# A graph layer's edge stream beside a state-space scan: PSUM banks regrouped, decays written to PSUM, row sums issued behind the turn and spread

## The chip, the cores and the metric

The kernel runs on one core of one Trainium2 chip. The metric is the device time of one launch in microseconds (us). The kernel before takes 3823.23 us, the median of 3 runs (3822.45 to 3824.71).

## What is computed

`x` is 6250 nodes by 256 features, with 200,000 edges (`src`, `dst`, sorted by `dst`). One graph layer and one mixture-of-experts layer follow each other, each with a residual. The change concerns the first layer only:

```
xn   = layernorm(x)
proj = (xn @ gat_w.T).reshape(n, 4, 64)
e    = leaky_relu(s_src[src] + s_tgt[dst], 0.2)       # four heads
exp_e= exp(e - max(e)); denom = segment_sum(exp_e, dst)
agg  = segment_sum(proj[src] * exp_e / denom[dst], dst)
perm = argsort(out_degree(src) + noise)
xz   = xn[perm] @ in_proj.T                           # -> xc, z
xc   = silu(causal_conv4(xc)); dbc = xc @ x_proj.T    # dt row, B, C
dt   = softplus(dt_row @ dt_proj.T + b)
h_t  = exp(dt * A) * h_(t-1) + (dt * xc) * B_t        # 256 channels x 16 states
y    = (h * C).sum(states) + xc * D_param;  y = y * silu(z) @ out_proj.T
```

After it come the per-node part (norms, gate, feed-forward) and the experts (`nodes`, `plan`, `experts`), which the change leaves as they are.

## The kernel before

`layers` runs two streams of work at once on the same engines.

The **edge stream** goes by *pairs* (an edge chunk of 512 edges and a tile of 128 target nodes), 440 in all. For a pair, GpSimd (POOL) issues four indirect DMAs (`gather`, L567) that bring 4 x 128 rows of 260 numbers into `G`. ScalarE (ACT) makes the one-hot of the targets (`one_hot`, L628 and L633). TensorE (PE) turns it (`turn`, L663) and spreads the tile's scores over the edges (`spread`, L670), both into PSUM bank `fl_ptx`; ACT copies them out (`keep_turned`, L643 and L644). Every fourth pair VectorE (DVE) makes the logits of four pairs (`logits`, L585 to L602), and ACT their exponentials: into the rows in SBUF (`weights`, L648) and into PSUM bank `fl_pw` (`weights_again`, L654). DVE multiplies the gathered rows by them (`scale`, L610), PE sums them per target (`gather_sums`, L683, four matmuls, eight records in the trace, into one of two banks `fl_ps0`, `fl_ps1`), and DVE adds the sum to `ACC` (`add`, L620). POOL may gather pair q once the sums of pair q-8 are made (`free`).

The **scan stream** goes by *chunks* of 224 nodes, 28 in all. A chunk has 16 *slots*, one per state. Two neighbouring states are handled together. DVE forms the inflow in the odd slot before (`inflow`, L1111, reading PSUM bank `fl_pb`), scans both states in the even slot (`scan`, L1124: 900 elements of decays `mb_dA` and inflows `mb_dB`, both in SBUF) and multiplies by C in the odd slot (`read_out`, L1134, reading `fl_pc`). ACT makes the decays of one state per slot (`decay`, L1251: two activations of 224), two states ahead, in a buffer for four states. PE copies B and C to all partitions (`copies_b` L1353 in odd slots, `copies_c` L1363 in even slots) and sums over the states (`sum_up`, L1375, odd slots).

Three slots of every four (1, 2, 3, 5, 6, 7, 9, 10, 11, 13, 14, 15 of a chunk) carry a pair; slots 0, 4, 8, 12 carry none. The logits fall in slots 1, 6 and 11. Beside that each slot prepares a part of the next chunk (`prepare`) or gives out the last (`give_out`): PE has in slot 2 the projection of z (L1382), in slot 4 the convolution (L1407), in slot 6 x_proj, in slot 8 dt, in slot 10 the output projection.

The order on each engine is written out by hand: `run` calls each engine's own `slot(M, S)` for 32 slots (two chunks), and then loops over 32-slot bodies. Every engine works through its queue in order; the engines meet through counting semaphores (`s["turned_sb"]`, `s["added"]` and so on). The edge stream starts earlier, beside the counting of degrees (36 pairs) and the ranking (56 pairs), and has 12 more pairs before the first chunk's scan.

What is handed to PE in a slot, in the kernel before, is the body of

```
def edges_tensor(pe, S):
    if not early(S.number, 2):
        gather_sums(pe, S - 2)
    turn(pe, S + GU)
    spread(pe, S + GU)
```

## Time and profile before

| | |
|---|---|
| median of 3 runs | 3823.23 us (3822.45 to 3824.71) |
| the profiled execution | 3830.27 us, its span 3828.5 us |
| busy share of the span | PE 76%, PEld 56%, DVE 70%, ACT 57%, POOL 69% |
| busy in 915 to 2868 us, the 28 chunks (1953 us) | PE 1618.89, DVE 1732.35, ACT 1406.68, POOL 1542.10 us |
| mean granted TensorE clock | 0.898 in the whole, 0.96 in that stretch |

How to read it: PEld is TensorE's loading of weights, which lies beside the matmuls. Idle time stands behind an instruction in brackets, with the event that ended it. The chain that ended last names only the experts at the end of the program, so for the stretch of the scans the engines' idle times and the timeline have to be read. POOL's spans are rough, but the starts of its instructions follow each other closely enough to be counted.

### The profile page before, as it was taken

To read this page: it belongs to the slowest core of one execution; us is meant where nothing else is said; L and a number is where in the kernel's file an instruction comes from. 1 tells how busy PE (TensorE), PEld (TensorE's weight loads), DVE (VectorE), ACT (ScalarE), POOL (GpSimd) and SP (SyncE) were. 2 spreads that over 40 slices of the span, in tenths; PEclk is the share of its full clock that TensorE was granted. 3 is DMA by queue.
4 is the path that set the end of the run, shared out by engine and by line. 5 is a ranking of instruction groups with operands and counts; after the bars stand their busy time and mean duration, and the time that the engine had idled before them with its cause. 6 is when DMAs were issued, how large, how long until landed. Compare 5 with 4: busy or idle time off the path is not lost. (4 is left out here: it accounts for less than half of the span.)

```text
span 3828.5 us, 60997 instructions
## 1 busy us (share of the span) xinstructions
PE 2897.5 (76%) x16306; PEld 2157.1 (56%) x16307; DVE 2661.2 (70%) x4225; ACT 2163.9 (57%) x4819; POOL 2649.2 (69%) x2119
## 2 busy tenths in 40 slices
PE   6465566517888788887888888888883889659998
PEld 5455455415565565565665655656652455448887
DVE  6577466625988988989888888899893788511111
ACT  2322377716777677777676776777772665412222
POOL 2788788877777777777777777777773477424443
PEclk9788777768899999999999999999996999879999
DMA  7333444454444444544444444444465243157775
GB/s 225 105 83 84 133 106 107 115 172 131 118 124 121 124 118 117 127 120 122 124 118 120 123 118 126 121 120 124 120 112 136 56 106 99 69 133 143 143 144 105
DMA packets 295783, 460.78 MB, mean 120 GB/s; under 512 B 59431, under 2 KB 217880, under 8 KB 295288
## 3 DMA queue, kind: packets, MB, share of 16 engines
q0 software_dynamic: 116320, 279.61, 30.8%
q1 hardware_dynamic: 179224, 178.73, 16.6%
q14 instruction: 180, 1.47, 0.1%
q8 instruction: 59, 0.97, 0.1%
HBM read 394.01 MB, written 63.43 MB: 119 GB/s over the span
## 5 line engine op out<-in xcount | busy, mean ns | idle before, releaser
L567 POOL DMA_INDIRECT el_g<-table,el_ix x1344 | 1546.7, 1151 | 412.4 <-issue 392.9
L683 PE MATMUL fl_ps<-el_g,el_oh 128*128 128x260 f32 x3520 | 959.0, 420 | 255.2 <-DVE el_g L610 207.2
L683 PEld LDWEIGHTS fl_ps<-el_g,el_oh 128*128 128x128 f32 x3520 | 697.3, 209 | 370.5 <-DVE el_g L610 215.1
L567 POOL DMA_INDIRECT el_g<-table,eg_src x436 | 592.8, 1360 | 155.2 <-issue 125.9
L610 DVE TENSOR_TENSOR el_g<-el_g,fl_pw 128x1024 f32<-128x1024 f32 x440 | 533.5, 1213 | 22.2 <-ACT fl_pw L654 22.1
L1124 DVE TENSOR_TENSOR_SCAN mb_h<-mb_dA,mb_zero,mb_dB 128x900 f32<-128x900 f32 x224 | 468.1, 2090 | 51.2 <-ACT mb_dA L1251 30.7
L1375 PE MATMUL fl_py<-mb_hc,ident 128*128 128x448 f32 x896 | 405.0, 576 | 0.5 <-DVE mb_hc L1134 0.5
L1251 ACT ACTIVATE mb_dA<-mb_dt,mb_a 128x224 f32<-128x224 f32 x900 | 382.7, 475 | 35.3 <-issue 21.2
L628 ACT ACTIVATE el_away<-el_dst,el_less 128x512 bf16<-128x512 bf16 x445 | 321.1, 721 | 108.3 <-DMA el_dst<-dst_rows 81.3
L2258 POOL DMA_INDIRECT out<-ex_y,ex_to x112 | 174.2, 1555 | 279.3 <-DVE ex_y L2217 254.5
L643 ACT CAST el_oh<-fl_ptx 128x512 f32<-128x512 bf16 x444 | 253.6, 571 | 190.8 <-PE fl_ptx L670 185.6
L663 PE MATMUL fl_ptx<-el_ident,el_oht 128*128 128x128 bf16 x1776 | 183.9, 230 | 183.3 <-ACT el_sx L644 167.3
L633 ACT ACTIVATE el_oht<-el_away 128x512 bf16<-128x512 bf16 x445 | 280.3, 630 | 36.2 <-issue 5.4
L663 PEld LDWEIGHTS fl_ptx<-el_ident,el_oht 128*128 128x128 bf16 x1776 | 139.5, 103 | 283.4 <-issue 155.0
L1111 DVE TENSOR_TENSOR mb_dB<-mb_u,fl_pb 128x896 f32<-128x896 f32 x225 | 242.5, 1078 | 46.8 <-PE fl_pb L1353 46.8
L2217 DVE TENSOR_TENSOR ex_y<-ex_py,ex_b 128x512 f32<-128x512 f32 x56 | 38.8, 692 | 333.0 <-PE ex_py L2179 333.0
L648 ACT ACTIVATE el_g<-el_dm 128x64 f32<-128x64 f32 x110 | 28.2, 256 | 424.6 <-DVE el_dm L601 424.4
L620 DVE TENSOR_TENSOR ACC<-ACC,fl_ps 128x260 f32 x440 | 182.7, 415 | 115.9 <-PE fl_ps L683 78.1
L1134 DVE TENSOR_TENSOR mb_hc<-mb_h,fl_pc 128x896 f32<-128x896 f32 x224 | 241.6, 1078 | 0.0
L585 DVE TENSOR_REDUCE el_s<-el_sx 128x128 f32<-128x384 f32 x110 | 67.6, 615 | 233.7 <-DMA el_g<-table,eg_src 171.3
L2232 ACT COPY ex_xt<-ex_px 128x512 f32<-128x512 f32 x56 | 32.8, 586 | 345.2 <-PE ex_px L2153 345.2
L1363 PE MATMUL fl_pc<-mb_parts,mb_sel 96*128 96x224 bf16 x448 | 84.9, 272 | 167.0 <-DVE mb_hc L1134 167.0
(306 smaller groups left out, 5509.0 us busy)
## 6 DMA issues: line engine op xcount, KB each, us to landing
el_dst<-dst_rows SPq DMA_DIRECT2D x446, 128.0 KB, 3.4
ex_w<-in_moe_W SPq DMA_DIRECT2D x56, 512.0 KB, 3.4
el_g<-table,el_ix POOLq DMA_INDIRECT x1344, 3.0
ex_x<-routed_x SPq DMA_DIRECT2D x56, 257.0 KB, 2.8
el_g<-table,eg_src POOLq DMA_INDIRECT x436, 2.8
mb_x<-sorted_x SPq DMA_DIRECT2D x30, 224.0 KB
table<-px_tr SPq DMA_DIRECT2D x7, 910.0 KB, 9.6
el_g<-in_x SPq DMA_DIRECT2D x7, 896.0 KB, 8.0
```

The source lines that it names most:

```text
L567: pool.indirect_dma_start(out=G[b // GU][:, b % GU * NJ + j, :], out_offset=None, in_=dram["table"], in_offset=bass.IndirectOffsetOnAxis(a ...
L610: nc.vector.tensor_tensor(rows, rows, weight[:, at, :].unsqueeze(3).to_broadcast([P, NJ, NH, FO]), ALU.mult).then_inc(s["scaled"], 1)
L628: nc.scalar.activation(AWAY[:], DST[:, n % 4, :], ACT.Abs, bias=LESS[:, 0:1]).then_inc(s["away"], 1)
L633: nc.scalar.activation(OHT[:, n % RO, :], AWAY[:], ACT.Relu, bias=1.0, scale=-1.0).then_inc(s["hot"], 1)
L643: nc.scalar.copy(OH[:, n % (2 * GU)], pT)
L663: nc.tensor.transpose(pT[:, j, :], OHT[:, n % RO, j * P:(j + 1) * P], I16[:])
L683: mm = nc.tensor.matmul(pS[n % 2], OH[:, n % (2 * GU), j, :], G[n // GU % 2][:, n % GU * NJ + j, :], start=j == 0, stop=j == NJ - 1)
L1111: nc.vector.tensor_tensor(dB[:, :, :, 1:], wide_u, pB[:].unsqueeze(2).to_broadcast([P, 2, KD, TC]), ALU.mult).then_inc(s["dB"], 1)
L1124: nc.vector.tensor_tensor_scan(line(H[:]), line(dA[:, n % 2 * 2:n % 2 * 2 + 2]), line(dB[:]), ZERO[:, 0:1], ALU.mult, ALU.add).then_inc(s[ ...
L1134: nc.vector.tensor_tensor(HC[:, n % 2], H[:, :, :, 1:], pC[:].unsqueeze(2).to_broadcast([P, 2, KD, TC]), ALU.mult).then_inc(s["hc"], 1)
L1251: ins = nc.scalar.activation(dA[:, n % 4, k, 1:], DT[:, n // NS % 2, k, :], ACT.Exp, scale=A[:, k, n % NS:n % NS + 1])
L1375: mm = nc.tensor.matmul(pY[:], w["ident"][:], HC[:, n % 2, r], start=first and r == 0, stop=last and r == 1)
```

## The change

- **Decays in PSUM.** The SBUF buffer `mb_dA` for four states goes. The decays of the two states of a scan are written by ACT to `pA`, two PSUM banks (`fl_pa`), with no second buffer. ACT therefore makes all four activations in the odd slot, behind `keep_last` and the slot's `prepare`, and waits for the scan before to be done. In even slots it makes none.
- **Banks.** `fl_ps0` and `fl_ps1` become one bank `fl_ps`, so the sums of a pair wait until the pair before has been added to `ACC`. The copies of C and the edge weights share `fl_pw`. PE, ACT and DVE are kept from touching this bank at the same time by waits: `copies_c` waits for the scaling (and in slot 12 for `weights_again`), `scale` in odd slots waits for the copies of C, `weights_again` waits for `read_out` or `copies_c`.
- **Order on PE.** `gather_sums` goes behind `turn` and `spread`; `copies_c` goes to the end of the even slot's edge work.
- The convolution taps, which lay in the buffer of the decays, have their own (`mb_taps`).

```diff
@@ -550,9 +550,9 @@
         pTX, words = ps("fl_ptx", [P, 512]), NJ * P // 2
         pT = pTX[:, 0:words].bitcast(BF16).rearrange("p (j e) -> p j e", e=P)
         pX = pTX[:, words:words + NJ * SPREAD].rearrange("p (j s) -> p j s", s=SPREAD)
-        pS = [ps(f"fl_ps{b}", [P, 512])[:, 0:ROW] for b in range(2)]
+        pS = ps("fl_ps", [P, 512])[:, 0:ROW]
         pW = ps("fl_pw", [P, 512])
-        weight = pW[:, 0:GU * NJ * NH].rearrange("p (c h) -> p c h", h=NH)
+        weight = pW[:, 2 * TC:2 * TC + GU * NJ * NH].rearrange("p (c h) -> p c h", h=NH)
         ACC = w["ACC"]
 
         def free(pool, p):
@@ -617,7 +617,7 @@
             if not early(q, 1):
                 dve.wait_ge(s["added"], q)
             dve.wait_ge(s["summed"], q + 1)
-            nc.vector.tensor_tensor(at, at, pS[p.n % 2], ALU.add).then_inc(s["added"], 1)
+            nc.vector.tensor_tensor(at, at, pS, ALU.add).then_inc(s["added"], 1)
 
         def one_hot(act, p):
 
@@ -676,11 +676,11 @@
             q, n = p.number, p.n
             pe.wait_ge(s["scaled"], q + 1)
             pe.wait_ge(s["turned_sb"], q + 1)
-            if not early(q, 2):
-
-                pe.wait_ge(s["added"], q - 1)
+            if not early(q, 1):
+
+                pe.wait_ge(s["added"], q)
             for j in range(NJ):
-                mm = nc.tensor.matmul(pS[n % 2], OH[:, n % (2 * GU), j, :], G[n // GU % 2][:, n % GU * NJ + j, :],
+                mm = nc.tensor.matmul(pS, OH[:, n % (2 * GU), j, :], G[n // GU % 2][:, n % GU * NJ + j, :],
                                       start=j == 0, stop=j == NJ - 1)
             mm.then_inc(s["summed"], 1)
 
@@ -700,10 +700,10 @@
                 weights_again(act, S)
 
         def edges_tensor(pe, S):
+            turn(pe, S + GU)
+            spread(pe, S + GU)
             if not early(S.number, 2):
                 gather_sums(pe, S - 2)
-            turn(pe, S + GU)
-            spread(pe, S + GU)
 
         with part:
             sb = lambda n, s_, t=F32: part.enter_context(nc.sbuf_tensor(n, s_, t))
@@ -940,15 +940,15 @@
             PARTS, MID = sb("mb_parts", [3 * 2 * NS, 2, TC], BF16), sb("mb_mid", [2 * NS, TC], BF16)
             REST = sb("mb_rest", [2 * NS, TC])
             DTR = sb("mb_dtr", [BX, TC])
-            dA = sb("mb_dA", [P, 4, KD, 1 + TC])
             dB, H = (sb(f"mb_{n}", [P, 2, KD, 1 + TC]) for n in ("dB", "h"))
             HC = sb("mb_hc", [P, 2, 2, KD, TC])
-            taps = dA[:].rearrange("p b k t -> p (b k t)")[:, 0:CONV * D].rearrange("p (j d) -> p j d", j=CONV)
+            taps = sb("mb_taps", [P, CONV, D])[:]
             XN = [t.rearrange("p b k t -> p (b k t)")[:, u * D:(u + 1) * D] for t in (dB[:], H[:], HC[:, 0]) for u in range(3)]
             H0, ZERO = sb("mb_h0", [P, N2, 2, KD]), sb("mb_zero", [P, 1])
             LOWER = sb("mb_lower", [P, 1])
             Y, O, OR = sb("mb_y", [P, KD, TC]), sb("mb_o", [P, KD, TC]), sb("mb_or", [RB, TS, D])
-            pB, pC = ps("fl_pb", [P, 2, TC]), ps("fl_pc", [P, 2, TC])
+            pB, pC = ps("fl_pb", [P, 2, TC]), pW[:, 0:2 * TC].rearrange("p (r t) -> p r t", r=2)
+            pA = ps("fl_pa", [P, 1024])[:, 0:2 * KD * (1 + TC)].rearrange("p (s k t) -> p s k t", s=2, k=KD)
             pY, pM = ps("fl_py", [P, KD, TC]), ps("fl_pm", [P, 512])
             wide = lambda t: t[:, 0:KD * TC].rearrange("p (k t) -> p k t", k=KD)
             xs = dram["sorted_x"].rearrange("(c r p) d -> c p r d", p=RB, r=TS)
@@ -1098,7 +1098,7 @@
                 dve.wait_ge(s["set"], 11)
 
                 nc.vector.memset(LOWER[:], float(-np.log(ROOT)))
-                nc.vector.memset(dA[:, :, :, 0:1], 0.0).then_inc(s["set"], 1)
+                nc.vector.memset(pA[:, :, :, 0:1], 0.0).then_inc(s["set"], 1)
 
                 def inflow(p):
 
@@ -1121,7 +1121,7 @@
                         dve.wait_ge(s["h0"], 2 * m)
                         dve.wait_ge(s["hc"], m)
                     line = lambda t: t.rearrange("p s k t -> p (s k t)")
-                    nc.vector.tensor_tensor_scan(line(H[:]), line(dA[:, n % 2 * 2:n % 2 * 2 + 2]), line(dB[:]), ZERO[:, 0:1],
+                    nc.vector.tensor_tensor_scan(line(H[:]), line(pA), line(dB[:]), ZERO[:, 0:1],
                                                  ALU.mult, ALU.add).then_inc(s["h"], 1)
 
                 def read_out(p):
@@ -1131,7 +1131,7 @@
                     if not early(m, 2):
 
                         dve.wait_ge(s["y"], m - 1)
-                    nc.vector.tensor_tensor(HC[:, n % 2], H[:, :, :, 1:], pC[:].unsqueeze(2).to_broadcast([P, 2, KD, TC]), ALU.mult
+                    nc.vector.tensor_tensor(HC[:, n % 2], H[:, :, :, 1:], pC.unsqueeze(2).to_broadcast([P, 2, KD, TC]), ALU.mult
                                             ).then_inc(s["hc"], 1)
 
                 def prepare(c, b, at):
@@ -1190,6 +1190,8 @@
                         give_out(c - 1, 1 - b)
                     if S:
                         add(dve, S - 3)
+                        if at % 2:
+                            dve.wait_ge(s["C"], two.number + 1)
                         scale(dve, S - 1)
                     steps = logits(dve, S) if S and S.n % GU == 0 else None
                     if steps:
@@ -1244,11 +1246,11 @@
                 def decay(p):
 
                     m, n = p.number, p.n
-                    if not early(m, 4):
-
-                        act.wait_ge(s["h"], two_states(p).number - 1)
+                    if not early(m, 2):
+
+                        act.wait_ge(s["h"], two_states(p).number)
                     for k in range(KD):
-                        ins = nc.scalar.activation(dA[:, n % 4, k, 1:], DT[:, n // NS % 2, k, :], ACT.Exp,
+                        ins = nc.scalar.activation(pA[:, n % 2, k, 1:], DT[:, n // NS % 2, k, :], ACT.Exp,
                                                    scale=A[:, k, n % NS:n % NS + 1])
                     ins.then_inc(s["dA"], 1)
 
@@ -1318,10 +1320,14 @@
                     if not early(c, 1):
                         give_out(c - 1, at)
                     prepare(c + 1, 1 - b, at)
-                    decay(M + 2)
+                    if at % 2:
+                        decay(M + 1)
+                        decay(M + 2)
                     if S:
                         keep_turned(act, S + GU)
                     if S and S.n % GU == 0:
+
+                        act.wait_ge(s["hc"] if at % 2 else s["C"], two_states(M).number + 1)
                         weights_again(act, S)
 
                 for k in range(SCAT):
@@ -1443,10 +1449,16 @@
                     two = two_states(M)
                     if at % 2:
                         copies_b(two + 1)
-                    else:
-                        copies_c(two)
                     if S:
                         edges_tensor(pe, S)
+                    if not at % 2:
+
+                        last = S or pair_beside(M - 1)
+                        pe.wait_ge(s["scaled"], last.number)
+                        if not S and last.n % GU == 0:
+
+                            pe.wait_ge(s["weight"], last.of(GU) + 1)
+                        copies_c(two)
                     if at % 2 and not early(M.number, 2):
                         sum_up(two - 1)
                     if not early(c, 1):
```

PE's queue in slot 2 of a chunk, in the kernel before, from the sums to the copies of B of slot 3 (`fl_ps` sums, `fl_ptx` turn and spread, `fl_pm` the projection of z, `fl_pb` copies of B):

```order
L683 MATMUL fl_ps<-el_g,el_oh 128x260 x4
L658 REGISTER_ALU
L663 MATMUL fl_ptx<-el_ident,el_oht 128x128 x4
L668 ISA
L668 TENSOR_LOAD eg_tile
L668 ISA x2
L670 ISA
L670 MATMUL fl_ptx<-eg_parts,el_oht 128x25 x4
L1382 MATMUL fl_pm<-mb_xt,mb_wi 128x224 x4
L1351 REGISTER_ALU
L1353 MATMUL fl_pb<-mb_parts,mb_sel 128x224 x2
```

The same place in the changed kernel, from slot 2's turn to the projection of z (`fl_pw` is now the copies of C):

```order
L663 MATMUL fl_ptx<-el_ident,el_oht 128x128 x4
L668 ISA
L668 TENSOR_LOAD eg_tile
L668 ISA x2
L670 ISA
L670 MATMUL fl_ptx<-eg_parts,el_oht 128x25 x4
L677 REGISTER_ALU
L683 MATMUL fl_ps<-el_g,el_oh 128x260 x4
L1457 REGISTER_ALU
L1369 MATMUL fl_pw<-mb_parts,mb_sel 128x224 x2
L1388 MATMUL fl_pm<-mb_xt,mb_wi 128x224 x4
```

The sums have moved from ahead of the turn to behind the spread, and the copies of C have moved in behind them, ahead of the projection.

ACT's queue in slots 2 and 3, in the kernel before (`el_away`, `el_oht` one-hot; `el_oh`, `el_sx` the copies of turn and spread; `mb_sz` the copy of z):

```order
L628 ACTIVATE el_away<-el_dst,el_less 128x512
L633 ACTIVATE el_oht<-el_away 128x512
L1251 ACTIVATE mb_dA<-mb_dt,mb_a 128x224 x2
L643 CAST el_oh<-fl_ptx 128x512
L644 COPY el_sx<-fl_ptx 128x100
L628 ACTIVATE el_away<-el_dst,el_less 128x512
L633 ACTIVATE el_oht<-el_away 128x512
L1239 COPY mb_h<-mb_h 128x4
L1242 COPY mb_dB<-mb_h 128x4
L1266 COPY mb_sz<-fl_pm 128x448
L1251 ACTIVATE mb_dA<-mb_dt,mb_a 128x224 x2
```

The same place in the changed kernel:

```order
L628 ACTIVATE el_away<-el_dst,el_less 128x512
L633 ACTIVATE el_oht<-el_away 128x512
L643 CAST el_oh<-fl_ptx 128x512
L644 COPY el_sx<-fl_ptx 128x100
L628 ACTIVATE el_away<-el_dst,el_less 128x512
L633 ACTIVATE el_oht<-el_away 128x512
L1241 COPY mb_h<-mb_h 128x4
L1244 COPY mb_dB<-mb_h 128x4
L1268 COPY mb_sz<-fl_pm 128x448
L1253 ACTIVATE fl_pa<-mb_dt,mb_a 128x224 x4
```

Slot 2 has lost its two activations of decays, and slot 3 has four, ahead of the copies of turn and spread.

## Rows read from the trace of the kernel before

**Rows 1.** Busy time by engine in the chunks' stretch: PE, PEld, DVE, ACT, POOL, clock, DMA

```profile
915.00:2868.00 1953.00, 1618.89 (x8927) 1169.88 (x8926) 1732.35 (x2291) 1406.68 (x3439) 1542.10 (x1340) 0.96 0.48 121
```

**Rows 2.** Groups by line, same stretch: count, busy us, mean ns, idle before

```profile
L567 POOL DMA_INDIRECT el_g<-table,el_ix x1339 | 1542.0, 1152 | 410.9 <-issue 391.4 <-PE fl_ps L683 19.5
...
L1124 DVE TENSOR_TENSOR_SCAN mb_h<-mb_dA,mb_zero,mb_dB 128x900 f32<-128x900 f32 x224 | 468.1, 2090 | 51.2 <-ACT mb_dA L1251 30.7 <-DVE mb_dB L1111 18.0 <-issue 2.3
...
L585 DVE TENSOR_REDUCE el_s<-el_sx 128x128 f32<-128x384 f32 x84 | 51.6, 615 | 23.1 <-ACT el_sx L644 14.6 <-DMA el_g<-table,el_ix 8.3
...
L1165 DVE SCALAR_TENSOR_TENSOR mb_dt<-mb_v,mb_t 128x448 f32<-128x448 f32 x28 | 17.5, 625 | 1.0
```

**Rows 3.** Timeline, a gather beside a scan and one alone: start, duration, engine

```profile
2025.38 2.08 DVE L1124 TENSOR_TENSOR_SCAN mb_h<-mb_dA,mb_zero,mb_dB 128x900 f32<-128x900 f32 x1
2025.51 2.71 POOL L567 DMA_INDIRECT el_g<-table,el_ix  x1 [0.30 <-PE fl_ps L683]
...
2028.52 0.95 POOL L567 DMA_INDIRECT el_g<-table,el_ix  x1 [0.30 <-issue]
```

**Rows 4.** Groups by line, POOL beside the ranking, 440 to 760 us

```profile
L567 POOL DMA_INDIRECT el_g<-table,eg_src x205 | 257.4, 1256 | 64.1 <-issue 58.5 <-PE fl_ps L683 5.6
```

**Rows 5.** Timeline, slots 0 to 6 of one chunk, three engines

```profile
2102.13 2.09 DVE L1124 TENSOR_TENSOR_SCAN mb_h<-mb_dA,mb_zero,mb_dB 128x900 f32<-128x900 f32 x1 [0.23 <-DVE mb_dB L1111]
...
2107.78 1.93 PE L683 MATMUL fl_ps<-el_g,el_oh 128*128 128x260 f32 x8
...
2108.31 0.26 ACT L648 ACTIVATE el_g<-el_dm 128x64 f32<-128x64 f32 x1 [3.64 <-DVE el_dm L601]
...
2109.11 0.85 ACT L1251 ACTIVATE mb_dA<-mb_dt,mb_a 128x224 f32<-128x224 f32 x2
...
2109.87 0.57 ACT L643 CAST el_oh<-fl_ptx 128x512 f32<-128x512 bf16 x1
...
2110.34 0.25 ACT L644 COPY el_sx<-fl_ptx 128x100 f32<-128x100 f32 x1
...
2110.47 0.24 ACT L654 ACTIVATE fl_pw<-el_dm 128x64 f32<-128x64 f32 x1
...
2110.73 0.38 PE L663 MATMUL fl_ptx<-el_ident,el_oht 128*128 128x128 bf16 x4 [1.01 <-ACT el_sx L644]
...
2117.38 2.45 PE L1407 MATMUL fl_pm<-mb_xt,mb_wc 128*128 128x224 f32 x12
...
2123.64 1.93 PE L683 MATMUL fl_ps<-el_g,el_oh 128*128 128x260 f32 x8
...
2123.84 1.09 DVE L1111 TENSOR_TENSOR mb_dB<-mb_u,fl_pb 128x896 f32<-128x896 f32 x1 [0.98 <-PE fl_pb L1353]
...
2125.41 0.39 PE L663 MATMUL fl_ptx<-el_ident,el_oht 128*128 128x128 bf16 x4
...
2125.72 0.43 DVE L620 TENSOR_TENSOR ACC<-ACC,fl_ps 128x260 f32 x1 [0.79 <-PE fl_ps L683]
...
2127.43 0.24 ACT L644 COPY el_sx<-fl_ptx 128x100 f32<-128x100 f32 x1
...
2128.00 0.62 DVE L585 TENSOR_REDUCE el_s<-el_sx 128x128 f32<-128x384 f32 x1 [0.72 <-ACT el_sx L644]
```

**Rows 6.** Timeline, slots 7 and 8 of that chunk, and the next chunk's first scan

```profile
2133.42 1.22 DVE L610 TENSOR_TENSOR el_g<-el_g,fl_pw 128x1024 f32<-128x1024 f32 x1 [0.64 <-ACT fl_pw L654]
...
2137.13 0.85 ACT L1251 ACTIVATE mb_dA<-mb_dt,mb_a 128x224 f32<-128x224 f32 x2
...
2138.02 2.09 DVE L1124 TENSOR_TENSOR_SCAN mb_h<-mb_dA,mb_zero,mb_dB 128x900 f32<-128x900 f32 x1 [1.10 <-ACT mb_dA L1251]
...
2171.22 2.09 DVE L1124 TENSOR_TENSOR_SCAN mb_h<-mb_dA,mb_zero,mb_dB 128x900 f32<-128x900 f32 x1 [0.23 <-DVE mb_dB L1111]
```

**Rows 7.** Busy time by engine in 2042 to 2046 us, columns as in Rows 1

```profile
2042.00:2046.00 4.00, 4.00 (x14) 3.27 (x13) 4.00 (x4) 3.48 (x10) 3.33 (x3) 0.57 0.52 132
```

**Rows 8.** Timeline, the sums of slot 3 in that stretch

```profile
2043.88 2.74 PE L683 MATMUL fl_ps<-el_g,el_oh 128*128 128x260 f32 x8
```

## The prediction

> **What bounds the kernel now.** The chain of waits that ended last names only the experts' part, so I read the stretch of the 28 chunks by itself: first busy time by engine, then the groups by line, then the timeline of one chunk. The stretch takes 1953 us, 69.75 us a chunk; DVE is busy for 1732, POOL for 1542, PE for 1619, ACT for 1407 [rows 1].
>
> POOL looks like a bound. Its gathers take 1542.0 us and its gaps before them 410.9, together 1953, and nearly all gaps are "issue" [rows 2]: it never waits. A gather that starts beside a scan takes 2.71 us, one alone 0.95 [rows 3], so the mean of 1152 ns is 1339 x 0.2 = 270 us above one alone. The reader is to see that POOL is blocked by the scans, and that it has no idle time to give.
>
> The question is how much DVE waits for POOL. DVE's waits for gathered rows are at L585, and "DMA" has 8.3 us there in the whole stretch [rows 2]. The rest of DVE's idle time ends with PE or ACT, or is the short step from one instruction to the next. The quiet chunk of the timeline has none of those waits for DMA and lasts from 2102.13 to 2171.22, 69.09 us [rows 5, 6]. So there are two bounds almost in one place: POOL at 69.75, and the ring of DVE, PE and ACT at 69.1. Freeing POOL gives 28 x 0.66 = 18 us at most unless the ring also gets shorter. What the change does to the ring decides.
>
> **The ring, part by part.** Times are of the quiet chunk.
>
> *Slots 1 to 5, PE's order.* Before, the sums of slot 2 (2107.78, 1.93 us) run while ACT is still behind: PE then waits 1.01 us for ACT's copy, and turns at 2110.73 [rows 5]. From that turn to the convolution at 2117.38 and on to the sums at 2123.64 PE hardly rests, and the end of this stretch is waited for: DVE's inflow at 2123.84 had waited 0.98 us for the copies of B behind the convolution [rows 5]. Now the sums of slot 2 must follow the turn. So 1.93 us of work that lay in a pause goes into the stretch that is waited for; the next instruction starts 1.77 behind the start of such sums (2123.64 to 2125.41) [rows 5], and I take 1.8. The copies of C of slot 2 go in as well: 0.2 us (a start-to-start step, as from PE's copies of B to the sums). Slots 3 and 4 have the same work in another order.
>
> *Slots 1 to 5, ACT's order.* The turn waits for ACT's copy, which ended at 2110.34 + 0.25. In slot 1 ACT had one state's decays, 0.85 us busy, the next one starting 0.76 behind (2109.11 to 2109.87) [rows 5]. Now it has two states' there, all ahead of this copy: +0.8. Together the convolution and the inflow of slot 5 come 1.8 + 0.2 + 0.8 = 2.8 us later. Behind the inflow, which reads PSUM, are slot 6's `add`, `scale` and logits in DVE's queue, and PE's next copies of C.
>
> *Slot 6.* `add` waits for sums that now follow turn and spread: +0.3 (2125.41 to the next instruction on PE). But the later gate is the logits' wait for the copies of slot 5, which stand behind the second pair of decays: +0.8 again. The read at 2128.00 came 0.3 us after the copy's end (2127.43 + 0.24) [rows 5], and I take that off: +0.5.
>
> *Slot 7.* Decays no longer stand between the logits and the edge weights. DVE's 0.64 us wait there [rows 6] goes: -0.6.
>
> *Slot 8.* The scan waited 1.10 us for decays that began at 2137.13, behind slot 7's copies [rows 6]. Both pairs are now there: +0.8. The wait at slot 2's `scale` (a second pair of decays ahead of `weights_again`) is 0.3 and lies ahead of the stretch that PE sets, so it costs nothing.
>
> *Other slots.* In slots 3, 11, 13 and 15 ACT makes the four activations (twice 0.8 us) while DVE has at least `read_out` and inflow (1.09 each), and mostly `add` and `scale` too, so the single buffer costs nothing there. The wait of `scale` for the copies of C is met: PE needs about 2.2 us after `add` for sums and copies, and DVE has `scale` and a scan, 3.3 us, between. In slot 12 the copies wait for `weights_again`; DVE's scan covers it. POOL needs sums eight pairs back, and at over 70 us a chunk it has some 9 us of slack in each, so its wait for later sums costs nothing.
>
> *PSUM operands.* ACT's 64-element exponential takes 0.24 us into PSUM and 0.26 into SBUF [rows 5]; that is nothing to 0.02 per activation, and I take 0.1 off a chunk. The Trainium skill (ScalarE: Activation LUTs, Step-by-step: what each stage is for) says that writing to PSUM is faster than writing to SBUF, without a figure for it. The trace agrees in sign; by the rule alone the sum would be lower, by the row it is lower by this 0.1. The scan's price from PSUM isn't in the trace. A DVE operation with two SBUF inputs takes 625 ns for 448 elements, 1.4 ns each, and the inflow with one in PSUM 1.09 us for 896, 1.2 ns [rows 2, 5]; the scan has 2.3 ns [rows 2]. Below: the scan falls to the inflow's rate, -1.0 us each. Above: a fixed 0.23 us more, as one dependent step of DVE costs (2102.13) [rows 5], on the five scans of eight that the ring waits for: +1.2 a chunk. I take 0: L1165 with two SBUF inputs isn't slow, so the scan's 2.3 ns is its own, and reading PSUM shows no surcharge in the inflow.
>
> Sum: 2.8 + 0.5 - 0.6 + 0.8 - 0.1 = +3.4 on 69.1, thus 72.5. I leave in the low TensorE clock that chunks have at times (below), 0.66 less POOL's share of 8.3/28 = 0.3: 72.5 + 0.35 = 72.85, or +3.1 against 69.75. 28 x 3.1 = 87 us.
>
> *Before the chunks.* 104 pairs run with the single bank and the new order. Beside the ranking POOL takes 257.4 + 64.1 us of 320, 6.3 us a pair, and almost never waits for sums [rows 4]. It may run eight pairs ahead of them, so sums a few us later cost 0; at worst 0.1 us a pair, 10 us.
>
> The profiled execution takes 3830.3 us, so 3917 by its own measure; it stands 7 us above the median of the runs, which gives 3910.
>
> **Rivals.**
>
> *POOL's blockade was the real bound (faster).* With the scan's decays in PSUM, gathers fall towards 0.95 + 0.3 us: 48 x 1.25 = 60 us a chunk. The Trainium skill (SBUF — State Buffer, Who interferes with whom) says that a VectorE instruction with at most one SBUF input, outside its two-port modes, doesn't contend with GpSimd; rows 3 agree with a blockade by an operation that has two, and by that rule it ends. For this rival speaks that POOL is full. If the ring's costs are hidden, the chunk goes from 69.75 to 69.1 or a little lower: 3823 - 18 = 3805. Its far end is DVE's busy time plus half of its idle time, 1732 + 110 = 1842, or -111: 3712. It decides as soon as the ring grows by less than 0.6 us a chunk. Against it: DVE waited only 8.3 us for gathers, and two of my terms stand on waits that exist already (0.98 and 1.10 us).
>
> *The scan itself gets faster (faster).* At -1.0 us per scan, five of eight on the ring's path: 3.1 - 5 = -1.9 a chunk, 3823 - 53 = 3770. L1165 speaks against it.
>
> *PE's clock falls in the stretch that is waited for (slower still).* PE's pause ahead of slot 2's turn grows from 1.01 us to about 3, since the sums no longer fill it. In the chunk before the quiet one the granted clock had 0.57 of full speed at that place, near the lower of TensorE's levels (1.2 of 2.4 GHz) [rows 7], and the sums took 2.74 us instead of 1.93 [rows 8]. With 0.8 for the sums and as much for the projection before them in every chunk: 3.1 + 1.6 - 0.35 = 4.35, x 28 = 122: 3945. Against it: the quiet chunk had a pause too, and kept its clock.
>
> *Only ACT's part lands.* If PE catches up by slot 5, +0.5 - 0.6 + 0.8 + 0.8 = 1.5 less 0.7 that POOL gives: 0.8 a chunk, 3846.
>
> **How the numbers follow.** Forecast 50%; clock 20%; only ACT's part 10%; POOL's blockade 16% (4 of it within 0.2%); the faster scan 4%. The forecast's own range is 3880 to 3940, for the terms of 2.8 and 0.8 may together be off by a third. The range that leaves out 2 in 10 is 3815 to 3965. A measurement of this kernel tells 0.2%, about 8 us, from no change. Faster 17%, same 5%, slower 78%.
>
> **What would show it.** Right: gathers beside scans at 0.95 us and POOL waiting for sums; DVE's wait at the inflow for the copies of B near 3 to 4 us once a chunk; the scan's waits for decays near 1.6 to 2 us; no wait at `scale` in slot 7; PE's long pauses ahead of the turns; busy time of DVE unchanged. Wrong: L1111's wait below 1.5 us on average per chunk, a scan that isn't 2.09 us, or gathers still at 1152 ns. Less than 70 us between first scans of chunks would refute the whole reckoning.

## The result

The changed kernel takes 4007.18 us (median of 4 runs, 4004.43 to 4018.18) against 3823.44 for the kernel before in the same comparison: **ratio 1.0486, 95% interval 1.0466 to 1.0506**. A second comparison gave 1.0478 (1.0459 to 1.0497). It is slower, as forecast, but by 184 us where 87 were forecast, and beyond the range.

The first scan starts at 926.7 us (before 915.1) and the last at 3057.1 (before 2865.5): 11.6 us are lost ahead of the chunks, 180 in them. Busy time by engine in the chunks' stretch of the changed kernel, columns as in rows 1:

```profile
926.70:3067.50 2140.80, 1716.65 (x8951) 1280.21 (x8952) 1742.80 (x2296) 1408.12 (x3442) 1288.45 (x1345) 0.90 0.43 111
```

DVE and ACT have the work they had [rows 1], DVE with 10 us more in a longer stretch. POOL has 254 us less, and TensorE's mean clock is 0.90 where it was 0.96. The groups by line there (count, busy us, mean ns of one, then the idle time before them and what ended it):

```profile
L567 POOL DMA_INDIRECT el_g<-table,el_ix x1344 | 1287.5, 958 | 850.5 <-PE fl_ps L683 471.4 <-issue 379.1
L683 PE MATMUL fl_ps<-el_g,el_oh 128*128 128x260 f32 x2697 | 792.3, 444 | 148.9 <-DVE ACC L620 147.5
L1124 DVE TENSOR_TENSOR_SCAN mb_h<-fl_pa,mb_zero,mb_dB 128x900 f32<-128x900 f32 x224 | 467.7, 2088 | 74.6 <-ACT fl_pa L1253 55.4 <-DVE mb_dB L1111 15.5 <-issue 3.5
L610 DVE TENSOR_TENSOR el_g<-el_g,fl_pw 128x1024 f32<-128x1024 f32 x337 | 409.3, 1214 | 2.3 <-ACT fl_pw L654 2.0
L1111 DVE TENSOR_TENSOR mb_dB<-mb_u,fl_pb 128x896 f32<-128x896 f32 x224 | 241.7, 1079 | 102.6 <-PE fl_pb L1359 102.1
L620 DVE TENSOR_TENSOR ACC<-ACC,fl_ps 128x260 f32 x338 | 142.0, 420 | 175.3 <-PE fl_ps L683 127.7 <-issue 45.5
L585 DVE TENSOR_REDUCE el_s<-el_sx 128x128 f32<-128x384 f32 x84 | 51.5, 614 | 25.1 <-ACT el_sx L644 25.1
```

Beside rows 2: gathers fell from 1152 to 958 ns, the scan stayed at 2.09 us, and POOL waits 471 us for sums. None of DVE's waits in these rows ends with POOL or a gather. Its waits per chunk (the sums above divided by 28 chunks): 4.6 us for sums (L620), 3.6 for the copies of B (L1111), 2.0 for decays.

One chunk, slots 1 to 5, from slot 1's decays to the sums that slot 6 waits for (start, duration; scans at 2158.08 and 2165.40):

```profile
2154.57 1.56 ACT L1253 ACTIVATE fl_pa<-mb_dt,mb_a 128x224 f32<-128x224 f32 x4
2156.55 0.24 ACT L644 COPY el_sx<-fl_ptx 128x100 f32<-128x100 f32 x1
2156.93 0.38 PE L663 MATMUL fl_ptx<-el_ident,el_oht 128*128 128x128 bf16 x4 [3.35 <-ACT el_sx L644]
2158.05 3.42 PE L683 MATMUL fl_ps<-el_g,el_oh 128*128 128x260 f32 x8
2161.62 0.43 DVE L620 TENSOR_TENSOR ACC<-ACC,fl_ps 128x260 f32 x1 [1.45 <-PE fl_ps L683]
2162.26 0.94 POOL L567 DMA_INDIRECT el_g<-table,el_ix  x1 [2.71 <-PE fl_ps L683]
...
2167.09 2.45 PE L1413 MATMUL fl_pm<-mb_xt,mb_wc 128*128 128x224 f32 x12
...
2173.56 1.09 DVE L1111 TENSOR_TENSOR mb_dB<-mb_u,fl_pb 128x896 f32<-128x896 f32 x1 [3.62 <-PE fl_pb L1359]
2173.69 2.00 PE L683 MATMUL fl_ps<-el_g,el_oh 128*128 128x260 f32 x8
2175.84 0.42 DVE L620 TENSOR_TENSOR ACC<-ACC,fl_ps 128x260 f32 x1 [1.19 <-PE fl_ps L683]
```

The sums of slot 2 used to run before the turn, in ACT's shadow [rows 5]. Now PE stands 3.35 us, turns, and makes them in 3.42 us instead of 1.93: the add waits for them, and everything up to the convolution and the inflow of slot 5 comes later. Slots 8, 9 and 13:

```profile
2188.09 2.09 DVE L1124 TENSOR_TENSOR_SCAN mb_h<-fl_pa,mb_zero,mb_dB 128x900 f32<-128x900 f32 x1 [1.68 <-ACT fl_pa L1253]
2190.63 0.42 DVE L620 TENSOR_TENSOR ACC<-ACC,fl_ps 128x260 f32 x1
2191.20 3.36 PE L683 MATMUL fl_ps<-el_g,el_oh 128*128 128x260 f32 x8 [1.12 <-DVE ACC L620]
2194.71 0.42 DVE L620 TENSOR_TENSOR ACC<-ACC,fl_ps 128x260 f32 x1 [0.53 <-PE fl_ps L683]
...
2211.51 0.42 DVE L620 TENSOR_TENSOR ACC<-ACC,fl_ps 128x260 f32 x1 [0.67 <-issue]
2212.08 3.71 PE L683 MATMUL fl_ps<-el_g,el_oh 128*128 128x260 f32 x8 [3.47 <-DVE ACC L620]
2216.01 0.43 DVE L620 TENSOR_TENSOR ACC<-ACC,fl_ps 128x260 f32 x1 [0.95 <-PE fl_ps L683]
```

At both places PE stands waiting for the add, the bank being single, then sums slowly, and the next add waits in turn. The granted clock in the three stretches of slow sums (slots 2, 9 and 13; columns as in rows 1) is near half of full speed:

```profile
2158.00:2161.50 3.50, 3.50 (x14) 2.76 (x12) 2.17 (x2) 2.46 (x7) 1.24 (x2) 0.58 0.62 148
2191.20:2194.50 3.30, 3.30 (x9) 2.63 (x10) 2.98 (x3) 3.24 (x8) 1.16 (x2) 0.57 0.49 153
2212.10:2215.80 3.70, 3.70 (x9) 2.95 (x10) 2.96 (x3) 1.48 (x4) 0.00 (x0) 0.53 0.42 129
```

In 23 chunks in the middle of the stretch (the third to the 25th) 60 of 276 groups of sums are slow (above 2.4 us, against 2.0), 2.6 a chunk: those of slot 13 in all 23 chunks, those of slot 2 in 22, those of slot 9 in 13. In the one chunk in which slot 2's sums are fast (1.99 us), PE's pause ahead of the turn is 1.6 us, against 3.2 to 3.5 in the others. In the same chunks of the kernel before 21 groups are slow, 0.9 a chunk.

From scan to scan, the mean over the same 23 chunks, in us (g0 is from the scan of slot 0 to that of slot 2, g7 from the scan of slot 14 to the next chunk's first). The first two rows are of the first comparison, the others of experiments that ran on the same chip as the second:

| | g0 | g1 | g2 | g3 | g4 | g5 | g6 | g7 | chunk | ratio |
|---|---|---|---|---|---|---|---|---|---|---|
| before | 10.70 | 5.76 | 10.67 | 9.49 | 7.47 | 10.67 | 9.31 | 5.77 | 69.8 | 1 |
| changed | 10.48 | 7.71 | 13.46 | 9.38 | 7.89 | 10.54 | 10.57 | 6.41 | 76.4 | 1.0486 |
| order + single bank | 10.43 | 6.60 | 12.76 | 9.49 | 7.51 | 10.68 | 10.45 | 7.28 | 75.2 | 1.0368 |
| order + one buffer of decays | 10.48 | 8.19 | 13.50 | 9.64 | 7.47 | 10.69 | 9.32 | 5.76 | 75.1 | 1.0383 |
| changed, decays in SBUF | 10.48 | 7.76 | 13.48 | 9.51 | 7.92 | 10.68 | 10.49 | 6.52 | 76.8 | 1.0510 |

The experiments ran on four chips. On one the kernel before takes 3825 us, as in the first comparison; it is called the quiet chip. On the three others it takes 4024 to 4063 us, and all kernels traced there show waits that the quiet chip's traces don't have. Ratios are compared within one kind of chip only.

### The profile page after: what moved, and what is told of

It reads as the page before. It is cut to its first block and busy times, and to the rows that moved or that the text cites. A ratio compares the mean times of both kernels' runs of the same rounds, so it can differ in the third digit from the quotient of the medians.

```text
span 4016.4 us, 61437 instructions
## 1 busy us (share of the span) xinstructions
PE 2990.5 (74%) x16306; PEld 2260.7 (56%) x16307; DVE 2670.9 (66%) x4225; ACT 2162.4 (54%) x4819; POOL 2387.9 (59%) x2119
## 5 line engine op out<-in xcount | busy, mean ns | idle before, releaser
L567 POOL DMA_INDIRECT el_g<-table,el_ix x1344 | 1287.5, 958 | 850.5 <-PE fl_ps L683 471.4
L683 PE MATMUL fl_ps<-el_g,el_oh 128*128 128x260 f32 x3520 | 1058.6, 453 | 235.9 <-DVE ACC L620 231.6
L683 PEld LDWEIGHTS fl_ps<-el_g,el_oh 128*128 128x128 f32 x3520 | 744.4, 222 | 371.0 <-issue 227.9
L610 DVE TENSOR_TENSOR el_g<-el_g,fl_pw 128x1024 f32<-128x1024 f32 x440 | 534.2, 1214 | 2.8 <-ACT fl_pw L654 2.5
L1124 DVE TENSOR_TENSOR_SCAN mb_h<-fl_pa,mb_zero,mb_dB 128x900 f32<-128x900 f32 x224 | 467.7, 2088 | 74.6 <-ACT fl_pa L1253 55.4
L1381 PE MATMUL fl_py<-mb_hc,ident 128*128 128x448 f32 x896 | 389.1, 558 | 0.0
L620 DVE TENSOR_TENSOR ACC<-ACC,fl_ps 128x260 f32 x440 | 184.9, 420 | 276.2 <-PE fl_ps L683 225.2
L1253 ACT ACTIVATE fl_pa<-mb_dt,mb_a 128x224 f32<-128x224 f32 x900 | 350.8, 437 | 13.1 <-DVE mb_dt L1165 12.7
L1111 DVE TENSOR_TENSOR mb_dB<-mb_u,fl_pb 128x896 f32<-128x896 f32 x225 | 242.8, 1079 | 103.8 <-PE fl_pb L1359 103.4
L1381 PEld LDWEIGHTS fl_py<-mb_hc,ident 128*128 128x128 f32 x896 | 184.1, 206 | 109.1 <-issue 90.7
L1134 DVE TENSOR_TENSOR mb_hc<-mb_h,fl_pw 128x896 f32<-128x896 f32 x224 | 241.7, 1079 | 0.0
L2180 PE MATMUL ex_ph<-ex_xt,ex_w 128*128 128x256 f32 x896 | 204.6, 382 | 1.4 <-ACT ex_xt L2244 1.4
```

Source lines behind the costliest of these rows:

```text
L567: pool.indirect_dma_start(out=G[b // GU][:, b % GU * NJ + j, :], out_offset=None, in_=dram["table"], in_offset=bass.IndirectOffsetOnAxis(a ...
L610: nc.vector.tensor_tensor(rows, rows, weight[:, at, :].unsqueeze(3).to_broadcast([P, NJ, NH, FO]), ALU.mult).then_inc(s["scaled"], 1)
L683: mm = nc.tensor.matmul(pS, OH[:, n % (2 * GU), j, :], G[n // GU % 2][:, n % GU * NJ + j, :], start=j == 0, stop=j == NJ - 1)
L1111: nc.vector.tensor_tensor(dB[:, :, :, 1:], wide_u, pB[:].unsqueeze(2).to_broadcast([P, 2, KD, TC]), ALU.mult).then_inc(s["dB"], 1)
L1124: nc.vector.tensor_tensor_scan(line(H[:]), line(pA), line(dB[:]), ZERO[:, 0:1], ALU.mult, ALU.add).then_inc(s["h"], 1)
L1253: ins = nc.scalar.activation(pA[:, n % 2, k, 1:], DT[:, n // NS % 2, k, :], ACT.Exp, scale=A[:, k, n % NS:n % NS + 1])
```

## The experiments

### First, on another chip: one part at a time

The first four were compared with the kernel before at 4024 us, the last four with it at 4059 us on the same chip.

**Order alone** (`turn` and `spread` ahead of `gather_sums`, two banks, all else as before).

> The kernel before with one edit: the sums go behind turn and spread on PE (two banks for the sums, decays in SBUF as before). Theory A (the single bank is what costs: sums that may only start when the pair before has been added, at a TensorE clock that falls in the pause before them): with two banks the order alone costs the one sum that moves into the stretch up to the convolution, 1.8 us a chunk against 0.7 of slack, and some low clock: +30 to +60 us, 3855 to 3885; DVE's wait for sums stays near 1.1 us a chunk. Theory B (the order on PE is what costs): +120 to +190 us, 3945 to 4010.

Measured 1.0002 (0.9983 to 1.0022), below both theories. **One bank alone** (excerpt of the edit; the add reads the one bank too):

```diff
-                pe.wait_ge(s["added"], q - 1)
+                pe.wait_ge(s["added"], q)
-                mm = nc.tensor.matmul(pS[n % 2], OH[...
+                mm = nc.tensor.matmul(pS, OH[...
```

> The kernel before with one edit: one bank for the sums, the order on PE as before. Theory A: PE stands at the head of every slot until the pair before is added, then makes the sums and only then turns; +80 to +180 us, 3900 to 4000, with waits of PE for ACC near 6 us a chunk. Theory B: the bank alone costs little, 0 to +30 us, up to 3855.

Measured 1.0433 (1.0391 to 1.0475), in theory A's range. **C's copies in the weights' bank alone**, with the added waits:

> The kernel before with one edit: the copies of C share the bank of the edge weights, with the waits of the change (copies of C at the end of the even slot's edge work); two banks for the sums, old order of sums and turn, decays in SBUF. Theories A and B alike: 0 to +15 us, 3820 to 3840. Theory C (the waits between weights, scale and copies of C are what costs): +60 us or more, 3885 or above, with DVE waiting at the edge weights or PE at the copies of C.

Measured 1.0086 (1.0055 to 1.0117), between the theories and clear of no change. **Both states' decays in the odd slot, in one buffer in SBUF, alone** (excerpt):

```diff
-                    decay(M + 2)
+                    if at % 2:
+                        decay(M + 1)
+                        decay(M + 2)
```

> The kernel before with one edit: both decays of a pair in the odd slot into one buffer for two states, which stays in SBUF. By the prediction's terms for ACT's order: +0.8 ahead of slot 2's turn, +0.5 at the logits of slot 6, -0.6 at slot 7, +0.8 at slot 8, 1.5 us on 69.1 a chunk, less what POOL bounds anyway: +15 to +35 us, 3840 to 3860, gathers still at 1150 ns. Theory D (the decays' order is what costs): +100 us or more.

Measured 0.9968 (0.9944 to 0.9993), below both. Then parts taken out of the changed kernel. **Decays as before** (SBUF, four states, two ahead):

> The changed kernel with the decays put back: SBUF, four states, one state per slot two ahead (bank sharing, one bank for sums and the new order on PE stay). Theory A: most of the loss stays, since the single bank and the order do: 3960 to 3990, with DVE's waits for sums near 4 us a chunk. Theory D (decays are what costs): 3850 or below. Gathers are back at 1150 ns.

Measured 1.0188 (1.0158 to 1.0219), between the theories, and **the same with two banks for the sums**:

> The changed kernel with the decays put back as in e4_decays_back and two banks for the sums again (bank of C shared, new order on PE). Theory A: the sums no longer wait for the addition, and the loss falls to that of the order alone, 3855 to 3890. Theory B (order): still above 3940.

Measured 0.9999 (0.9979 to 1.0019), below both. **The old order in the changed kernel**:

> The changed kernel with one edit undone: the sums come ahead of turn and spread again, with the single bank. Theory A: with one bank neither order helps, since PE now stands ahead of the turn until the addition is done: 3990 to 4050. Theory B: the order is the cause and undoing it wins most back: below 3900.

Measured 1.0800 (1.0754 to 1.0846), above both. **TensorE's pauses filled** in the changed kernel, ahead of the sums of slots 2, 9 and 13 (excerpt):

```diff
+                    if at == 2:
+                        copies_b(two + 1, 8)
...
+                        if at in (9, 13):
+                            copies_b(two + 1, 4 if at == 9 else 14)
```

> The changed kernel with PE's pauses filled: the copies of B are repeated 8 times in slot 2 (for slot 3), 4 times in slot 9 and 14 times in slot 13, each ahead of the turn or the sums that PE would wait for; the same values are written, so nothing else changes. Theory A in its form with the clock: the sums run at full clock (1.93 instead of 3.4 us), DVE's wait for sums falls from 4.4 to about 1.5 us a chunk and the chunk from 76.4 to 73, thus 3905 to 3925. If the clock is only a companion and the handshake itself costs: 3985 to 4010.

Measured 1.0506 (1.0471 to 1.0541), just above both.

Read by themselves these say: the single bank costs 4%, the shared bank of C 1%, the order nothing. But the kernel before was 5 to 6% slower on this chip than in the first comparison, so a part could look free because it lay in time lost anyway. Such time is seen on a second of the other chips, in the kernel with the order alone:

```profile
1916.31 0.36 PE L1353 MATMUL fl_pb<-mb_parts,mb_sel 96*128 96x224 bf16 x2
...
1919.29 1.70 PE L683 MATMUL fl_ps<-el_g,el_oh 128*128 128x260 f32 x7 [0.78 <-issue]
1919.48 0.78 ACT L1270 ACTIVATE mb_xc<-fl_pm,mb_cb 128x224 f32<-128x224 f32 x2 [7.13 <-remote]
1919.52 1.09 DVE L1111 TENSOR_TENSOR mb_dB<-mb_u,fl_pb 128x896 f32<-128x896 f32 x1 [5.47 <-remote]
```

By its record the last copy of B ends at 1916.67, yet DVE goes on 2.8 us later, and ACT, which waits for the convolution (end of its record 1916.47), 3.0 us later. The profile calls the releaser "remote", since no instruction of the core ended shortly before. But both semaphores are raised by PE alone in this stretch, and the trace has them rise at 1919.46 and 1919.50. So it is PE's own signal that comes late, and its sums stand in the same stretch without a named releaser (0.78 us above). In this run 66 of the 200 recorded signals of the copies of B come over 0.5 us behind the end of their record, up to 8.7 us; in the kernel before on the quiet chip none of 222 does, the latest by 0.015 us. Why PE's signals come late on those chips stays open; the ends of matmuls are modelled in the profile, so it can't be told whether the matmuls themselves ran late.

### On the quiet chip (before: 3825 us)

**The changed kernel again:**

> The changed kernel as it is, beside the three others of this call, so that all parts have the whole as their measure on one chip. Theory S (the single bank of sums carries the cost, the other parts hold little): 1.02 to 1.035 of the kernel before. Theory M (the cost is a sum over the single bank and the decays' single buffer, each of which takes slack that the other would need): 1.045 to 1.06, as in the first comparison. If it comes out at 1.07 or above, the pauses filled in TensorE's order (ratio 1.0506 in its own call) did gain something; at 1.05 they gained nothing and the lower clock is not what costs.

1.0478 (1.0459 to 1.0497), in theory M's range. **Order and single bank together:**

> The kernel before with two of the four parts: one bank for the sums, and the sums behind turn and spread. The single bank alone in the old order was 1.043, the order alone 1.000. Theory S: the new order lies beside the handshake and hides a part of it, 1.015 to 1.025 (the step from two banks to one was 0.019 with all but the PSUM decays in place). Theory C (the clock falls wherever sums have to wait for the add, and that is what costs): the pauses stay, 1.035 to 1.045.

1.0368 (1.0351 to 1.0386), in theory C's range. **Order and the one buffer of decays, two banks:**

> The kernel before with the new order of TensorE and the decays of both states in the odd slot in one buffer in SBUF, two banks for the sums. Both parts alone were 1.000 and 0.997. Theory S: nothing in common between them, 0.995 to 1.000. Theory M (the parts take slack from each other): 1.01 to 1.02.

1.0383 (1.0366 to 1.0400), above both theories. **The changed kernel with its single buffer of decays in SBUF:**

> The changed kernel with the decays in one two-state buffer in SBUF instead of PSUM; order, waits and the single bank of sums as changed. With four states in SBUF and the old lead the ratio was 1.019. Theory M: the single buffer is what costs on top of the single bank, so this is as slow as the changed kernel or slower, since gathers and scan get in each other's way again: 1.045 to 1.065. Theory P (writing and reading PSUM, or the faster gathers, is what costs): 1.015 to 1.025.

1.0510 (1.0493 to 1.0528), in theory M's range.

Both pairs that share the new order cost 3.7 to 3.8%, and all parts 4.8. No part ran alone on this chip, and the shared bank of C ran there only with all the others. With order and one buffer (two banks) the loss lies in g1 and g2 alone, and g6 and g7 are as before (table). Slot 2 in that kernel, and below it the granted clock (0.50, the lower of TensorE's two levels, 1.2 of 2.4 GHz) while it sums:

```profile
1899.93 0.59 PE L663 MATMUL fl_ptx<-el_ident,el_oht 128*128 128x128 bf16 x4 [3.85 <-ACT el_sx L644]
1900.95 3.81 PE L683 MATMUL fl_ps<-el_g,el_oh 128*128 128x260 f32 x8
1904.56 2.56 PE L1384 MATMUL fl_pm<-mb_xt,mb_wi 128*128 128x224 f32 x8
1904.99 0.43 DVE L620 TENSOR_TENSOR ACC<-ACC,fl_ps 128x260 f32 x1 [1.81 <-PE fl_ps L683]
```

```profile
1901.00:1904.70 3.70, 3.70 (x13) 2.93 (x11) 2.17 (x2) 2.42 (x7) 3.09 (x3) 0.50 0.46 122
```

PE doesn't wait for an add in it. The pause of 3.85 us comes from the order and from ACT's second pair of decays; the sums behind it take 3.81 us, twice the usual time, and the projection 2.56 instead of 1.7. In the kernel with order and single bank, which has no second pair of decays there, the pause is 2.4 us in the mean, and the sums behind it are still slow in all 23 chunks (3.0 to 3.8 us). So with the new order the sums of slot 2 are slow with either number of banks.

Slot 13 with two banks (order and one buffer). The first lines are of a usual chunk, the last three of one of the 3 chunks in 23 in which its sums are slow:

```profile
2027.19 1.99 PE L683 MATMUL fl_ps<-el_g,el_oh 128*128 128x260 f32 x8
2029.96 0.43 DVE L620 TENSOR_TENSOR ACC<-ACC,fl_ps 128x260 f32 x1 [0.32 <-issue]
...
1952.47 3.81 PE L683 MATMUL fl_ps<-el_g,el_oh 128*128 128x260 f32 x8
...
1955.20 0.43 DVE L620 TENSOR_TENSOR ACC<-ACC,fl_ps 128x260 f32 x1 [0.32 <-issue]
1958.67 0.42 DVE L620 TENSOR_TENSOR ACC<-ACC,fl_ps 128x260 f32 x1
```

The same slot with one bank (order and single bank), where its sums are slow in all 23 chunks:

```profile
1958.89 0.43 DVE L620 TENSOR_TENSOR ACC<-ACC,fl_ps 128x260 f32 x1 [0.32 <-issue]
1959.46 3.80 PE L683 MATMUL fl_ps<-el_g,el_oh 128*128 128x260 f32 x8 [3.77 <-DVE ACC L620]
1963.48 0.43 DVE L620 TENSOR_TENSOR ACC<-ACC,fl_ps 128x260 f32 x1 [1.04 <-PE fl_ps L683]
```

With two banks the sums start 2.7 us before the add of the pair ahead, and even where they are slow they are done when their own add comes. With one they may start only after that add. So PE stands 3.77 us for it, and the sums behind this pause are slow. In the two-bank chunk the next add comes 3.5 us behind the one ahead with nothing in the way (1955.20 to 1958.67), which holds sums of 2.0 us and not sums of 3.8. So the single bank makes the pause, and by these timelines it takes the low clock behind it as well to make the next add late. With the bank alone, in the old order on the other chips, slot 13's sums are slow in all 27 chunks counted, with the order alone there in 0, 0 and 1 of 27. No kernel here has a single bank and fast sums in that slot without added work.

### The parts again, and fills

**Order, bank, one buffer and filled pauses** once more, each by itself, on one of the other chips (before: 4063 us).

> The kernel before with the sums behind turn and spread, nothing else (two banks, decays and copies of C as before). On a chip where the kernel before ran 5% slower it came out at 1.000; on the chip that ran both kernels as at first, this order with the decays' single buffer gave 1.038 and this order with the single bank 1.037. Theory O (the order carries most of the loss: the sums of slot 2 land behind TensorE's wait for slot 2's row numbers and run at the lower clock, 1.9 us for the add there, and in front of the awaited convolution they hold the copies of B 2.1 us more): chunks of 74.3 to 75.1 us against 69.8, ratio 1.03 to 1.038. Theory H (the handshake on one bank or the single buffer of decays carries it, and the order only where one of them is there): 1.000 to 1.01.

> The kernel before with one bank for the sums in the old order. Theory H2 (the add waits at three places, about slots 3, 13 and 15, as in the first run of it, where the ratio was 1.043): 1.035 to 1.045. Theory O: with the sums ahead of turn and spread the handshake costs what it added to the new order, no more than 2.6 us per chunk in slots 13 to 15: 1.01 to 1.02.

> The kernel before with both states' decays in the odd slot into one buffer in SBUF. The first run of it, on the slower chip, gave 0.997. Theory of the prediction (only ACT's order costs, 0.8 us per chunk before the scan of slot 9): 1.005 to 1.012. If there is a gain in it: 0.99 to 0.998.

> The changed kernel with TensorE's pauses before the sums of slots 2, 9 and 13 filled by copies of B made again (8, 4 and 14 times), so that the clock should not fall there; changed kernel here 1.048. Theory C (part of the loss is the lower clock: slot 2's sums take 1.99 us instead of 3.2 to 3.8 and the add there waits no more, 1.6 us, and up to 2 us at the other two places): chunks of 73 to 75 us, ratio 1.02 to 1.035. Theory N (the sums are late by their place in the order and by the handshake, whatever the clock): 1.045 to 1.055.

Measured 0.9967 (0.9942 to 0.9993), 1.0357 (1.0293 to 1.0420), 0.9971 (0.9941 to 1.0001) and 1.0456 (1.0396 to 1.0515): just below theory H, in the range of theory H2, in that of a gain, and in theory N's. **The order a third time**, again on a chip where the kernel before takes 4058 us, so by its expectation there is no verdict from the ratio:

> TensorE's order alone once more, for a chip on which the kernel before takes about 3825 us. Theory O: chunks of 74.3 to 75.1 us, the add of slot 2 waits 0.7 to 1.9 us, the copies of B of slot 4 are waited for 3.7 us against 1.5, ratio 1.03 to 1.038. Theory H: 1.000 to 1.01. If the kernel before takes above 4000 us again, no verdict from its ratio.

Measured 0.9973 (0.9953 to 0.9993). The three traces of the order alone do answer in part. In the first, 14 of 27 chunks take 73.9 to 74.7 us and the others more; this is one in which DVE and ACT have no wait for "remote" (1560.89 to 1634.93, 74.04 us):

```profile
1569.49 0.58 PE L663 MATMUL fl_ptx<-el_ident,el_oht 128*128 128x128 bf16 x4 [3.11 <-issue]
1570.67 3.83 PE L683 MATMUL fl_ps<-el_g,el_oh 128*128 128x260 f32 x8
1574.65 0.43 DVE L620 TENSOR_TENSOR ACC<-ACC,fl_ps 128x260 f32 x1 [1.24 <-PE fl_ps L683]
...
1587.57 1.09 DVE L1111 TENSOR_TENSOR mb_dB<-mb_u,fl_pb 128x896 f32<-128x896 f32 x1 [4.08 <-PE fl_pb L1353]
```

Its steps are g1 7.1 and g2 13.7, the rest within 0.3 us of before. PE turned 0.14 us behind the end of ACT's copy, so this is the wait for ACT, though the profile calls it "issue". The one chunk free of such waits in the second run takes 73.82. The order alone thus makes an undisturbed chunk of 69.1 us [rows 5, 6] one of about 74. Against the mean chunk of 69.8 us that is 4.1 us, and 28 x 4.1 = 115 us would be a ratio of 1.03 on the quiet chip: an estimate, for no run there has measured it. That its ratio on the other chips is 0.997 to 1.000 means that the kernel before loses about as much there. No trace of that kernel shows where. The nearest is the one buffer of decays alone, which keeps the old order and has nearly the same time: in its two traces g0 takes 13.2 and 13.6 us and g2 12.7 and 13.1 (means over 28 chunks), against 10.6 and 10.8 in the kernel before on the quiet chip, while g1, where the order alone has 6.8 to 7.3, takes 6.0.

**The changed kernel on such a chip** (before: 4058 us), as the measure of the parts taken out there:

> The changed kernel as it is, meant as the measure of the runs with one part undone where the kernel before takes above 4000 us. There, with the decays back in SBUF it was 1.019, with two banks as well 1.000, with the old order 1.080, with the pauses filled 1.051 and 1.046. If filling the pauses gains there (theory C, the lower clock costs), the changed kernel itself is at 1.06 or above; if it gains nothing (theory N), at 1.045 to 1.055. If the kernel before takes 3825 us here, 1.045 to 1.052 again.

Measured 1.0524 (1.0477 to 1.0570), in theory N's range. Filling the pauses (1.0506, 1.0456) gained nothing that can be told from this. But the fill reached its aim in one place of three. Slow sums in 27 chunks, changed kernel on such a chip against the two runs with the fill: slot 2, 9 against 5 and 9 (there it is slot 1 that is slow on those chips, 26 against 23 and 25); slot 9, 19 against 16 and 21; slot 13, 27 against 3 and 0. So in slot 13 the clock does follow the pause. The price is the time of the fill. This is one of the three chunks of the first run in which it stayed slow in part (sums of 2.59 us):

```profile
2110.14 5.39 PE L1359 MATMUL fl_pb<-mb_parts,mb_sel 96*128 96x224 bf16 x28
2112.05 0.43 DVE L620 TENSOR_TENSOR ACC<-ACC,fl_ps 128x260 f32 x1 [0.32 <-issue]
2115.33 2.59 PE L683 MATMUL fl_ps<-el_g,el_oh 128*128 128x260 f32 x8
2118.14 0.43 DVE L620 TENSOR_TENSOR ACC<-ACC,fl_ps 128x260 f32 x1 [1.48 <-PE fl_ps L683]
```

The copies took 5.39 us here and held up the sums by 2.8 us themselves. In the mean the sums of slot 13 start 1.4 us behind the add instead of 0.15 and take 2.0 us instead of 3.7: they are done 0.4 us sooner. So what the clock alone costs is not shown by an experiment.

With the old order and everything else changed (1.080) the kernel is slower than the changed one (1.052, on another chip): once there is a single bank, sums ahead of the turn make the turn wait for the add as well. PE waits 393 us for adds in the kernel with the bank alone, against 147.5 in the changed one. There the new order costs less than the old.

No kernel here beats the kernel before where it takes 3825 us. The one buffer of decays alone was 0.3% faster on two of the other chips, and in one of the two the interval leaves out 1; on the quiet chip it only ran together with the new order.

## Why the prediction was half right

Per chunk the forecast was +3.1 us and the chip gave 6.6 (76.4 against 69.8). The prediction's terms stood on one quiet chunk of 69.09 us [rows 5, 6], so they are held against that chunk here. The columns are the quiet chunk's times, the changed kernel's means over 23 chunks, the difference, and what was forecast for it, in us:

| | quiet chunk | changed | more | forecast |
|---|---|---|---|---|
| scan of slot 0 to turn of slot 2 | 8.60 | 9.29 | 0.7 | 0.8 |
| that turn to the convolution | 6.65 | 10.58 | 3.9 | 2.0 |
| convolution to the inflow of slot 5 | 6.46 | 6.47 | 0.0 | 0 |
| that inflow to the scan of slot 6 | 4.69 | 5.31 | 0.6 | 0.5 |
| to the scan of slot 8 (g3) | 9.49 | 9.38 | -0.1 | 0.2 |
| to the next chunk (g4 to g7) | 33.20 | 35.41 | 2.2 | 0 |
| chunk | 69.09 | 76.43 | 7.3 | 3.4 |

The forecast has 0.1 less for PSUM operands, in no one place. Two lines of the quiet chunk that this rests on, the projection of slot 2 and the scan of slot 6:

```profile
2111.71 1.76 PE L1382 MATMUL fl_pm<-mb_xt,mb_wi 128*128 128x224 f32 x8
...
2128.53 2.08 DVE L1124 TENSOR_TENSOR_SCAN mb_h<-mb_dA,mb_zero,mb_dB 128x900 f32<-128x900 f32 x1
```

- **ACT's order, +0.8 at the turn and +0.5 in slot 6: right** (0.7 and 0.6). The two pairs say the same: the turn comes 9.33 us behind the scan of slot 0 with order and one buffer, and 8.59 with order and single bank, whose ACT makes one state's decays there as before.
- **PE's order, +2.0: right, once the 1.9 us are taken off that the low clock adds (below).** The wait at the inflow was forecast at 3 to 4 us and is 3.62.
- **Slot 7, -0.6, and slot 8, +0.8: right in kind, together 0.3 too high.** The wait for weights at `scale` is gone (L610, 2.0 us in the whole stretch). The scan waits 1.68 us for decays instead of 1.10.
- **POOL's blockade, as a rival: the blockade went, and time did not come back.** Gathers fell to 958 ns, as the Trainium skill (SBUF — State Buffer, Who interferes with whom) has it for an operation with one SBUF input. The same kernel with decays in SBUF has gathers of 1170 ns and is 0.3% slower, the intervals just touching: that is all that the freed POOL was worth. The Trainium skill (ScalarE: Activation LUTs, Step-by-step: what each stage is for) has writes to PSUM faster; four activations in a row take 1.56 us there and 1.60 in SBUF, which agrees and is nothing. The scan takes 2.09 us from either, as taken.
- **The step that failed: "I leave in the low TensorE clock that chunks have at times", +0.35, and the single bank of sums left without any term.** Two things follow from it.
  - In slot 2 the pause ahead of the turn did grow to over 3 us, as the clock rival said, and the sums behind it ran at the low clock in 22 of 23 chunks, not at times. They take 3.54 us in the mean instead of 1.93 (+1.6), and the projection 2.00 instead of 1.76 (+0.2): that is the 1.9 us that the second row of the table has too much. The rival had +1.6 for both; its place and nearly its size were right, and it deserved the larger chance. Even so its 3945 us fell short, since it too had nothing for the bank.
  - In slots 9 and 13 to 15 it is the single bank: PE may not sum until the add is done, stands up to 3.5 us for it (slot 13), sums at the low clock, and the next add waits. g4 grew by 0.4, g6 and g7 together by 1.9. The prediction had a handshake between `add` and the next sums only for the copies of C, and there with sums of full speed (2.2 us for sums and copies against 3.3 between); sums of 3.4 to 3.8 us don't fit.
- Ahead of the chunks 0 was taken and 10 given as the worst; it was 11.6.

By kernels on the quiet chip: the single bank costs g6 and g7 +2.65 in the pair that has it and 0 in the pair that has not. What both pairs have, the order and slot 2's slow sums, is 2.7 us up to the scan of slot 6 in the first and 5.1 in the second, which has ACT's pair of decays and slower sums and projection too (3.82 and 2.49 us against 3.41 and 2.04). That the order with its slow sums holds about two thirds of the loss is an estimate from undisturbed chunks (4.8 of 7.3 us against the quiet chunk), not a ratio on that chip.

## What to carry to other kernels

Work that fills TensorE's pause can be paid for twice when it is moved behind the pause: once by its own length on the path, and once because the engine stood idle and, as here in nearly every chunk, comes back at the lower clock. Price a handshake on a single buffer with the slowest speed its producer shows in the trace, not with its mean. And measure one part at a time on the chip whose time for the kernel before is the one to be explained: where that kernel already loses 5%, a part that makes an undisturbed chunk 7% longer came out at nothing.
